# First-layer query and key projections: one ScalarE copy to SBUF, split on GpSimd, begun three steps sooner

## The reference

```python
x = x + _layernorm(_L0_attn_ref(_layernorm(x), wq, wk, wv, wo))      # 16 heads of 64, causal
x = x + _layernorm(_L0_ffn_ref(_layernorm(x), ...))                  # 8 experts, top 2, capacity
x = x + _layernorm(_L1_attn_ref(_layernorm(x), qkv, wo))             # 16 heads of 8, rotary, causal
x = x + _layernorm(_L1_ffn_ref(_layernorm(x), ...))                  # ternary weights, squared relu
```

## Time and profile before

| what | value |
|---|---|
| median of 3 runs | 1345.51 us (1344.99 to 1348.77) |
| the profiled execution: its own time | 1347.31 us |
| its span in the trace | 1345.5 us |
| PE busy | 1147.0 us, 85% |
| DVE busy | 938.8 us, 70% |
| ACT busy | 850.0 us, 63% |
| POOL busy | 122.8 us, 9% |
| mean granted clock of TensorE | 0.957 |
| first attention | 41 to 635 us of the span |

### The profile page before, as it was taken

How to read it: one execution, slowest core, us unless ns; L and a number is a source line. 1 busy time by engine, 2 the same in 40 slices (tenths; PEclk the granted TensorE clock), 3 DMA queues, 4 the chain that set the end, 5 groups by cost and what they waited for, 6 DMA issues and landing times.

```text
span 1345.5 us, 28730 instructions
## 1 busy us (share of the span) xinstructions
PE 1147.0 (85%) x10458; PEld 856.4 (64%) x10458; DVE 938.8 (70%) x2353; ACT 850.0 (63%) x1996; POOL 122.8 (9%) x105
## 2 busy tenths in 40 slices
PE   3699999989898989989989995188888888888886
PEld 1476767767676767767957773055655655656674
DVE  4466666666566666666543337589999899999953
ACT  2466666656666666665044332389989889999923
POOL 1600000000000000000400005100000000000033
PEclk9899999999999999999979997679999999999998
DMA  4212222221212222220100000422022022020001
GB/s 115 71 40 64 54 64 70 65 70 36 75 51 52 55 68 66 64 64 18 48 5 17 17 11 1 129 37 37 2 37 37 2 37 37 2 37 2 2 1 32
DMA packets 29672, 56.77 MB, mean 42 GB/s; under 512 B 4538, under 2 KB 14674, under 8 KB 29410
## 3 DMA queue, kind: packets, MB, share of 16 engines
q1 hardware_dynamic: 28738, 53.43, 17.4%
q10 hardware_dynamic: 800, 1.57, 0.4%
HBM read 25.49 MB, written 4.33 MB: 22 GB/s over the span
## 4 chain that ended last, share of the span: by engine, by line
PE 40%; DVE 26%; issue 18%; ACT 11%; DMA 3%; SPq 1%; POOL 1%; ACTq 0%; DVEq 0%; POOLq 0%
DVE Zb L787 9%; PE pT L1091 7%; PE pO L1032 7%; PE pS L1067 6%; ACT probs L574 4%; PE pS L1153 4%; DVE nmax L797 4%; PE pT L1165 3%; DVE Sm L801 3%; ACT PT L554 2%; PE pS L1114 2%; PE pT L994 2%; PE pT L998 2%; DVE Kl L737 1%; PE pS L1250 1%
## 5 line engine op out<-in xcount | busy, mean ns | idle before, releaser
L1091 PE MATMUL pT<-cst,probs 128*128 128x128 f32 x2304 | 374.0, 287 | 84.8 <-ACT probs L574 54.0
L1091 PEld LDWEIGHTS pT<-cst,probs 128*128 128x128 f32 x2304 | 248.9, 142 | 180.6 <-ACT probs L574 120.2
L574 ACT ACTIVATE probs<-pS,nmax 128x128 f32<-128x128 f32 (+7 forms) x256 | 190.1, 743 | 191.4 <-DVE nmax L797 157.9
L554 ACT COPY PT<-pT 128x512 f32<-128x512 f32 (+3 forms) x597 | 275.1, 483 | 12.8 <-PE pT L1091 11.3
L797 DVE TENSOR_REDUCE nmax<-pS 128x1 f32<-128x128 f32 (+7 forms) x256 | 192.1, 751 | 93.3 <-PE pS L1071 92.0
L1032 PE MATMUL pO<-PT,V 128*64 128x128 f32 (+1 forms) x4608 | 229.8, 276 | 7.9 <-issue 4.0
L574 ACT ACTIVATE probs<-Sm,nmax 128x128 f32<-128x128 f32 (+7 forms) x256 | 199.3, 778 | 28.6 <-DVE nmax L801 22.4
L787 DVE TENSOR_SCALAR Zb<-pS 128x128 bf16<-128x128 f32 (+7 forms) x256 | 192.8, 753 | 21.6 <-PE pS L1071 21.5
L1032 PEld LDWEIGHTS pO<-PT,V 128*64 128x64 f32 (+1 forms) x4608 | 179.9, 113 | 27.4 <-issue 6.5
L801 DVE CUSTOM_DVE_ANT_0 Sm<-pS,Zb 128x128 f32<-128x128 f32 (+7 forms) x256 | 193.4, 756 | 4.5
L1067 PE MATMUL pS<-Kh,Qs 128*128 128x512 f32 (+2 forms) x384 | 174.7, 459 | 7.1 <-DMA Kl<-Kl 6.9
(11 more groups left out here) (177 smaller groups left out, 1270.9 us busy)
## 6 DMA issues: line engine op xcount, KB each, us to landing
Qs<-Ql SPq DMA_DIRECT2D x32, 256.0 KB, 3.7
Kh<-Kh SPq DMA_DIRECT2D x32, 256.0 KB, 3.6
Kl<-Kl SPq DMA_DIRECT2D x32, 256.0 KB, 4.6
wq_t<-factors SPq DMA_DIRECT2D x32, 256.0 KB, 4.0
QS<-split SPq DMA_DIRECT2D x72, 64.0 KB
KS<-split SPq DMA_DIRECT2D x72, 64.0 KB
w0s<-in_w SPq DMA_DIRECT2D x8, 192.0 KB, 4.8
split<-parts SPq DMA_DIRECT2D x2, 768.0 KB, 3.5
```

The lines of the kernel that those rows point to most:

```text
L554: nc.scalar.copy(PT[:, g % 2, h, k0 * P:(k0 + nk) * P], pT[r % TBANKS][:, 0:nk * P])\
L574: nc.scalar.activation(probs[:, i % NPROB, 0:n], src[:, 0:n], ACT.Exp, bias=nmax[:, i % 4:i % 4 + 1], scale=sign, accum_out=total).then_in ...
L1091: m = nc.tensor.transpose(pT[r % TBANKS][:, kt * P:(kt + 1) * P], probs[:, item % NPROB, (k0 + kt) * P:(k0 + kt + 1) * P], ident)
```

## The change

Query and key projections other than those of (0, 0) are copied by ACT once, all 128 partitions together, into a new tile `raw` of two buffers (the scale of the queries is applied there). GpSimd makes the rounded number and the remainder from `raw`, two operations of 64 partitions each, and waits for each before the next (`split_step`). DVE no longer takes part, and `order_for_dve` is gone. Before ACT fills a buffer of `raw` again, it waits until GpSimd has finished the unit before the last. SP and the first scores of a half wait for `split_step` in place of DVE's count.

The projections of (c+1, 0) begin at step 17 instead of 20: steps 17, 19, 21, 23, 25, 27. With that the alternation of ACT and DVE for the transposed probabilities shifts in those steps. GpSimd's order is now: the split of (0, 1); the quantizing; then for each half the split of a later set followed by L498 for the half. `raw` lies in a region that grows by 4 KiB per partition, and two small tiles of the second layer (rdb, rs) move into it.

```diff
-                for c2, b2, start in ((c, 1, 1), (c + 1, 0, self.per // B + 4)):
+                for c2, b2, start in ((c, 1, 1), (c + 1, 0, self.per // B + 1)):
...
-        self.add(step, "P", (c, b, u // 2, u % 2), ["act"] if u // 2 == 2 else ["act", "dve"])
+        self.add(step, "P", (c, b, u // 2, u % 2), ["act", "dve"] if (c, b) == (0, 0) and u // 2 < 2 else ["act"])
...
+    def split_number(self, c, b, what, j):
+        return ((c * B + b) - 1) * 4 + what * 2 + j
...
+        raw = at(156, "raw", [P, 2, BANK])
...
# GpSimd
+            def split_projection(c, b):
+                for what in range(2):
+                    for j in range(2):
+                        number = plan.split_number(c, b, what, j)
+                        cols = slice(j * BANK, (j + 1) * BANK)
+                        source = raw[:, number % 2, :]
+                        rows = (slice(0, DH0), slice(DH0, P))
+                        high = [(Qs, Kh)[what][rows[h], b, h, cols] for h in range(HPC)]
+                        low = [Ql[rows[h], b, cols] if what == 0 else Kl[rows[h], b, h, cols] for h in range(HPC)]
+                        pool.wait_ge(A[0]["cp_act"], plan.projected(c, b, what, j, "act"))
+                        for h in range(HPC):
+                            pool.tensor_copy(high[h], source[rows[h], :]).then_inc(split_step, 1)
+                            pool.wait_ge(split_step, number * (2 * HPC) + h + 1)
+                        for h in range(HPC):
+                            i = pool.tensor_tensor(low[h], source[rows[h], :], high[h].bitcast(F32), ALU.subtract)
+                            i.then_inc(split_step, 1)
+                            pool.wait_ge(split_step, number * (2 * HPC) + HPC + h + 1)
+            pool.wait_ge(zeros_ready, 3)
+            split_projection(0, 1)
             pool.wait_ge(q_d, 4)
...
             for half in range(CH0 * B):
+                c, b = divmod(half, B)
+                if b == 0 and c + 1 < CH0:
+                    split_projection(c + 1, 0)
+                elif b == 1 and c + 1 < CH0:
+                    split_projection(c + 1, 1)
...
# ScalarE
+                if (c, b) != (0, 0) and what < 2:
+                    number = L[0].split_number(c, b, what, j)
+                    if number >= 2:
+                        act.wait_ge(split_step, 2 * HPC * (number - 1))
+                    i = nc.scalar.mul(raw[:, number % 2, :], p, DH0 ** -0.5 if what == 0 else 1.0)
...
# SyncE, before the query moves (and likewise before the key moves)
+                if (c, b) == (0, 0):
+                    sp.wait_ge(A[0]["cp_dve"], plan.projected(c, b, 0, 1, "dve"))
+                else:
+                    sp.wait_ge(split_step, 2 * HPC * (plan.split_number(c, b, 0, 1) + 1))
```

More of the change, by code:

```diff
@@ L56 @@
 KIB = 1024
-REGION = 156
+REGION = 160
 C_IDENT, C_CAUSAL, C_UPPER, C_IOTA, C_END = 0, 128, 256, 384, 392
@@ L226, in build @@
         parts = at(136, "parts", [P, 2, PARTS, S], BF16)
+        rdb = at(128, "rdb", [P, 2, P])
+        rs = at(129, "rs", [P, 2, P])
         xn = at(148, "xn", [P, NT, D])
@@ L249, in build @@
         rden = sb("rden", [P, 2, HPG])
-        rdb = sb("rdb", [P, 2, P])
-        rs = sb("rs", [P, 2, P])
         nmax = sb("nmax", [P, 4])
@@ L315, in build @@
         dens_inverted, turned, turned_copied, factors_out, factors_in, rescaled = (sem(n) for n in ("dens_inverted", "turned", "turned_copied", "factors_out", "factors_in", "rescaled"))
+        split_step = sem("split_step")
         names = ["s", "mx", "z", "p", "t", "cp_act", "cp_dve", "rd1", "rd", "o", "rs", "n"]
@@ L366, in halves @@
                 lo, hi = slice(0, DH0), slice(DH0, P)
-                sp.wait_ge(A[0]["cp_dve"], plan.projected(c, b, 0, 1, "dve"))
+                if (c, b) == (0, 0):
+                    sp.wait_ge(A[0]["cp_dve"], plan.projected(c, b, 0, 1, "dve"))
+                else:
+                    sp.wait_ge(split_step, 2 * HPC * (plan.split_number(c, b, 0, 1) + 1))
                 sp.dma_start(Qs[hi, b, 0, :].bitcast(F32), Ql[lo, b, :].bitcast(F32)).then_inc(ld_half[b], 16)
                 sp.dma_start(Qs[lo, b, 1, :].bitcast(F32), Ql[hi, b, :].bitcast(F32)).then_inc(ld_half[b], 16)
-                sp.wait_ge(A[0]["cp_dve"], plan.projected(c, b, 1, 1, "dve"))
+                if (c, b) == (0, 0):
+                    sp.wait_ge(A[0]["cp_dve"], plan.projected(c, b, 1, 1, "dve"))
+                else:
+                    sp.wait_ge(split_step, 2 * HPC * (plan.split_number(c, b, 1, 1) + 1))
                 for kx in (Kh, Kl):
@@ L487, in ternary @@
                 link(pool.tensor_scalar(w, t0, scale, None, ALU.mult))
+            plan = L[0]
+            def split_projection(c, b):
[17 more added lines that the diff above has]
+            split_projection(0, 1)
             pool.wait_ge(q_d, 4)
@@ L519, in projected @@
             def projected(a, args, p):
-                _, b, what, j = args
+                c, b, what, j = args
                 cols = slice(j * BANK, (j + 1) * BANK)
-                if what == 0:
+                if (c, b) != (0, 0) and what < 2:
[3 more added lines that the diff above has]
+                    i = nc.scalar.mul(raw[:, number % 2, :], p, DH0 ** -0.5 if what == 0 else 1.0)
+                elif what == 0:
                     nc.scalar.mul(Qs[0:DH0, b, 0, cols], p[0:DH0, :], DH0 ** -0.5)
@@ L820, in attention @@
                         spread(plan.group(i - 2))
-                    for r in plan.dve_at[i]:
+                    for r in plan.at_step[i]:
                         what, args, copies = plan.rounds[r]
-                        if what == "P":
-                            dve.wait_ge(a["cp_act"], copies["act"])
-                            projected(a, args, pT[r % TBANKS][:, :])
+                        if "dve" not in copies:
                             continue
@@ L1045, in attention @@
                         if k == 0 and i % (plan.per // B) == 0:
-                            for e2 in ("act", "dve"):
-                                pe.wait_ge(a["cp_" + e2], plan.projected(c, b, 1, 1, e2))
+                            if i == 0:
+                                for e2 in ("act", "dve"):
+                                    pe.wait_ge(a["cp_" + e2], plan.projected(c, b, 1, 1, e2))
+                            else:
+                                pe.wait_ge(split_step, 2 * HPC * (plan.split_number(c, b, 1, 1) + 1))
                             pe.wait_ge(ld_half[b], (c + 1) * (16 * 6))
```

## The result

The changed kernel takes 1282.81 us (median of 4, 1280.84 to 1288.6), the one before 1346.32 us (median of 4, 1344.99 to 1348.77). The ratio is 0.9524, with a 95% interval of 0.9497 to 0.9551. That is 63.5 us less. The forecast was 1300 us, 46 less, with a range that ended at 1290: the sign and the main cause were right, the size was not.

The account below looks back on a forecast made before the run. TensorE was taken to bound the first layer's attention, so only its waits could be won: 35 + 10 + 6 = 51 us, less 5 for late weights, 46 in all, giving 1300 us, range 1290 to 1335.

Parts of the forecast that it names:

- the 0.6 us left of a first half's 5.0: First halves (steps 0 to 16): 5.0 us of waits, 0.6 assumed to stay, so 8 x 4.4 = 35 us gained.
- the 1.4 us of a second half: Second halves (steps 16 to 31): waits of 1.4 us brought by six projections would go, 7 x 1.4 = 10 us.
- the 6 us for the clock: Step 5 of five turns: TensorE's granted clock drops after stalls; 5 x 1.6 = 8 us, of which 6 counted.
- the 5 us taken off for a late w0s: Step 17, turns 1 to 6: next turn's weights land 0.3 to 0.9 us late, 5 us lost in all.
- What bounds the kernel: First layer's attention, 41 to 635 us: TensorE, busy 551.7 of 594 us, bounds it; only its waits can be won.
- A copy ... I take 1.0: GpSimd's split units: a 64x512 copy takes 1.0 us, so a unit takes 4.9, at the ends 3.4 and 6.1.
- all waits gone: Lower end of the forecast range for the whole kernel: 1290 us.
- GpSimd does set the pace: Rival: copies of 1.6 us or more, units of 6.1, make keys and weights late: 1354; chance 0.15 including being disturbed.
- Half late: Rival: copies of about 1.3 us, units of 5.5, keys 1.1 and w0s 1.6 late: about 1314; chance 0.15.
- The waits were hidden anyway: Rival: TensorE waits for ACT's probabilities in the same steps, only 15 to 25 us come: 1325; chance 0.08.
- DVE and GpSimd did not disturb each other: Rival that they do disturb each other, looking like GpSimd setting the pace; chance 0.15 shared with that rival.

## Why the prediction was wrong in size

The steps that failed are four terms of the sum, all cut or priced too far to one side: the 0.6 us left of a first half's 5.0, the 1.4 us of a second half, the 6 us for the clock, and the 5 us taken off for a late w0s. What each measured follows.

*What bounds the kernel: right.* TensorE did, by what made it wait, and the step markers predicted the new steps well: 1.79, 2.82, 1.09 and 3.17 us for steps 3, 5, 8 and 9, against 1.9, 2.9, 1.1 and 3.3.

*"I leave 0.6 us of the 5.0": mis-sized.* A first half lost 5.12 us of waits, and nothing was left: 8 x (5.12 - 4.4) = 6 us. The estimate of the whole, 5.0, was close; the reserve had no row behind it. Steps 3, 5, 8 and 9 gained 4.64 us, where the forecast's own numbers for them give 4.3; steps 4 and 7, for which it named no gain, gave 0.29 and 0.19 more.

*"7 x 1.4" for the second halves: a cause was missing.* They gave 13.6 us and not 10. The 1.4 us of waits behind projections went as forecast: in turn 3 the six projections cost 6.63 us before and 5.24 in the changed kernel. What came on top lies in steps 18 (0.37 us) and 31 (0.16 to 0.41). The comparison with the last turn could not show it: step 18 loses the same time there, with no projection near, and the window ended at the marker of step 31. The start alone brings 1.6 us a turn, so three quarters of what a second half gained come with the move, which the forecast had as room for GpSimd only; 1.0 of it is waits for the bank that the split would have removed as well.

*The clock: counted short.* 6 us were taken for five drops. Those of turns 2, 3, 4 and 6 cost 6.6 us and are all gone, and turn 0's first half gave 2.3 more: 8.8. Some of this is luck, since the same waits brought a drop in some turns and not in others. The Trainium skill ("TensorE: Matmul & The Clock Gate", HAM oscillation) ties such drops to TensorE's idle gaps; the run with the old start agrees in part. Five turns fell to 0.50 right behind a wait of 2.2 to 2.6 us, shorter than those in the Trainium skill's own example, and two with such a wait did not.

*"A copy ... I take 1.0" and "5 us in all" for w0s: mis-sized, and the term that changed the sum most after the first halves.* The copy took 0.61 us, the unit 4.05 and not 4.9, the weights landed 2 us early, and the wait was nothing. The deadline itself was placed rightly: 1.4 us more per unit bring the waits for keys and weights. The bounds of 0.20 and 1.57 us held the copy, but 1.0 was a middle, not a reading. The Trainium skill ("GPSIMD Engine Reference", Engine selection) calls one-input work there roughly line-rate. The run shows 608 ns for 512 elements of a copy, near that, and 1.57 us for a compare with one input, far from it.

Together 6 + 4 + 3 + 5 = 18 us, the gap between 46 and 63.5. The range failed with them: its lower end took 51 to 55 us as "all waits gone", a sum from which the reserve of the first halves had already been cut. With the forecast's own terms uncut it is 8 x 5 + 7 x 1.4 + 8 = 58, or 1288, and that would still have ended 5 us above the result; the 4 us of steps 18 and 31 were in none of its rows.

*The rivals.* None came true. GpSimd does set the pace from somewhere between 5.4 and 6.8 us a unit, as placed (6.1 was the point given). Half late, put at 1314 with units of 5.5 us, is close to the run with two more copies, 1311.8 with 5.4, though 10 of its 25 us in the stage came from turn 0. "The waits were hidden anyway" is out, since TensorE has a matmul in flight in all but 0.8 us of the stage. DVE and GpSimd did not disturb each other in the changed kernel, where DVE's work comes out of PSUM: its maxima average 754 ns over the kernel, 751 before, with GpSimd busy for 283 us of the stage. The rival is real for operations out of SBUF, as the run with the split on DVE shows.

*Not settled:* how the 5.12 us of a first half divide. Held banks cost at least 1.6, with a hold shorter than before, and ACT's second copy 0.65, both measured in the changed kernel; the rest, at most 2.9, is put down to DVE's queue by difference, and the run with the split on DVE shows only that this wait is there and steep. These parts need not add. Why steps 31 became shorter, and why a clock drop follows one wait and not the next, stays open. No version tried beats the changed kernel. TensorE's matmuls leave no gap there, but its weight loads still wait 14 us in the stage for the exponentials' results, and whether that could be won no run shows.

## What to carry to other kernels

Work that stands in an engine's queue ahead of an operation on the critical chain can cost much of its own length, even when the engine is idle a third of the time: 9 us of it in a first half cost 6.5 us and a clock drop. An idle engine that sits on no chain can take it at almost three times the duration (4.05 us a unit against 1.4 on DVE, with the rounding taken over from ACT) and still win, if the moved work starts early enough and has two buffers. Place work that is free in time, like a projection, into steps in which the bound engine waits for another anyway. And when a sum of gains is cut by reserves, the end of the range has to be the uncut sum, with room for a term that no row shows.

## What the runs showed of the hardware

- GpSimd: a 64x512 copy with rounding to fp32r took 0.61 us, a 64x512 subtraction 1.27 us, the same as one of 128x512; a compare with one input of 128x512 takes 1.57. The number of inputs does not order them.
- DVE: the same copy from SBUF took 0.43 us and the subtraction 0.70 (0.86 and 1.41 for two) where GpSimd was idle, so GpSimd needs 1.4 and 1.8 times as long.
- DVE and GpSimd: when both worked out of SBUF, a DVE operation of 0.42 or 0.69 us took 2.5 to 2.9 us, and was through only after GpSimd's multiplication of 2.4 us. DVE's maxima, which read PSUM, were not slowed (754 ns against 751).
- TensorE's clock: behind five of seven waits of 2.2 to 2.6 us at a turn's start it was granted its lower level, 1.2 GHz, at a price of 1.6 us a turn. In the kernel before, the waits of steps 3 and 5, 0.9 to 1.2 us, were followed by it in five of eight turns. The one wait left between the changed kernel's turns, 0.5 us, brought none.
